# Weights of the later layers prepared within tiles 0 to 5, and rows of x loaded for the keys from GpSimd's queue

## The reference

```python
q = (x @ w_q.T).reshape(B, S, 16, 16); k = x @ w_k.T; v = x @ w_v.T      # one key and value head
attn = softmax(einsum('bshd,btd->bhst', q, k) * softmax_scale)
x = ln(x + einsum('bhst,btd->bshd', attn, v).reshape(B, S, D) @ w_out.T)
x = ln(x + gelu(x @ ternary(W1).T + b1) @ ternary(W2).T + b2)            # F = 1024; ternary: sign beyond half of mean |w|
xn = ln(x) * norm_g + norm_b; A = sigmoid(A_log)
states = A**t * cumsum((xn @ B_w.T + B_b) / max(A**t, 1e-8)); u = states @ C_w.T + C_b
h = scan over s: cat = [u_s, h]; ff1, ff2 = tanh(..); t = sigmoid(0.1 * ta + tb); h = ff1 * (1 - t) + t * ff2
x = ln(x + (x + h @ out_w.T + out_b))
x = ln(x + fp6_blocks(x) @ fp6_blocks(ffn_w).T + ffn_bias)
```

## Time and profile before

| | |
|---|---|
| median of 3 runs | 1734.12 us (1729.36 to 1743.55) |
| profiled execution | 1731.95 us, span 1730.2 us |
| busy in the span | PE 1595.8, DVE 1314.6, ACT 1240.9, POOL 1083.1 us |
| mean granted TensorE clock | 0.961 of full |
| first exponential of tiles 0, 1, 2, 3, 4, 5 | 99.1, 126.1, 146.4, 165.9, 186.1, 206.7 us |
| tiles from 12 on | 23.6 us each |

### The profile page before, as it was taken

How to read it: one execution, slowest core, us unless ns; L and a number is a source line. 1 busy time by engine, 2 the same in 40 slices (tenths; PEclk the granted TensorE clock), 3 DMA queues, 4 the chain that set the end, 5 groups by cost and what they waited for, 6 DMA issues and landing times.

```text
span 1730.2 us, 78853 instructions
## 1 busy us (share of the span) xinstructions
PE 1595.8 (92%) x32657; PEld 1129.0 (65%) x32657; DVE 1314.6 (76%) x2549; ACT 1240.9 (72%) x2343; POOL 1083.1 (63%) x3296
## 2 busy tenths in 40 slices
PE   5869989999999999999999999999999999998665
PEld 4635656676777677777667777677777677766542
DVE  5547777788888888888888888888888888884654
ACT  3426777777788777787777787777888777877321
POOL 5001235677777777777777777777777777777532
PEclk8869999999999999999999999999999999999965
DMA  9965444344433444433344433444433344420010
GB/s 235 189 91 68 63 65 59 45 73 76 76 68 63 62 75 76 75 64 61 68 76 76 75 65 58 70 75 76 76 65 62 66 76 76 76 46 22 24 30 19
DMA packets 133676, 123.75 MB, mean 72 GB/s; under 512 B 19157, under 2 KB 130825, under 8 KB 133321
## 3 DMA queue, kind: packets, MB, share of 16 engines
q1 hardware_dynamic: 129120, 118.45, 39.7%
q10 hardware_dynamic: 4200, 0.27, 0.2%
HBM read 33.73 MB, written 17.83 MB: 30 GB/s over the span
## 4 chain that ended last, share of the span: by engine, by line
PE 58%; ACT 24%; issue 5%; DVE 4%; DMA 4%; SPq 3%; POOL 2%; ACTq 0%; DVEq 0%; POOLq 0%
PE value_bank L908 11%; PE gen_bank L726 10%; PE score_banks L886 10%; ACT probs L1265 6%; PE gen_bank L733 6%; PE gate_bank L941 5%; PE max_banks L716 5%; ACT hT L1248 5%; ACT L1265 4%; ACT L1248 4%; PE gen_bank L724 3%; ACT hhi L1253 2%; ACT x L1198 2%; PE gen_bank L960 2%; PE gen_bank L950 1%
## 5 line engine op out<-in xcount | busy, mean ns | idle before, releaser
L1317 DVE TENSOR_REDUCE nmax<-max_banks 128x2 f32<-128x1024 f32 x512 | 620.7, 1212 | 77.7 <-PE max_banks L718 76.0
L1265 ACT ACTIVATE probs<-score_banks 128x1024 f32<-128x1024 f32 x512 | 522.7, 1021 | 135.1 <-PE score_banks L888 112.1
L908 PE MATMUL value_bank<-probs,vaug 128*32 128x128 f32 x8192 | 327.0, 278 | 1.6 <-ACT probs L1265 1.1
L908 PEld LDWEIGHTS value_bank<-probs,vaug 128*32 128x32 f32 x8192 | 212.6, 110 | 96.6 <-issue 74.1
L886 PE MATMUL score_banks<-qaug,kaug 64*128 64x512 f32 x512 | 249.5, 487 | 24.1 <-ACT probs L1265 17.9
L888 PE MATMUL score_banks<-qaug,kaug 64*128 64x512 f32 x512 | 249.5, 487 | 0.0
L716 PE MATMUL max_banks<-kaug,qaug 62*128 62x512 f32 x512 | 227.3, 444 | 18.6 <-DVE nmax L1317 6.6
L718 PE MATMUL max_banks<-kaug,qaug 62*128 62x512 f32 x512 | 227.4, 444 | 2.7 <-issue 2.7
L1836 POOL TENSOR_TENSOR diff<-gates 128x16 f32<-128x16 f32 x448 | 100.1, 224 | 199.3 <-ACT gates L1271 198.8
L941 PEld LDWEIGHTS gate_bank<-hseq,ghT 128*32 128x32 f32 x10944 | 141.1, 112 | 63.3 <-POOL hseq L1841 35.6
L941 PE MATMUL gate_bank<-hseq,ghT 128*32 128x16 f32 x10944 | 171.2, 185 | 3.8 <-DVE hseq L1452 1.8
(11 more groups left out here) (228 smaller groups left out, 3591.7 us busy)
## 6 DMA issues: line engine op xcount, KB each, us to landing
qstage<-qhalf SPq DMA_DIRECT2D x384, 128.0 KB
qstage<-qhalf SPq DMA_DIRECT2D x128, 112.0 KB
xt<-in_L_attn_x SPq DMA_DIRECT2D x64, 128.0 KB
xk<-in_L_attn_x SPq DMA_DIRECT2D x16, 512.0 KB, 8.2
residual<-x2s SPq DMA_DIRECT2D x64, 128.0 KB
x2f<-residual SPq DMA_DIRECT2D x64, 128.0 KB
out<-x SPq DMA_DIRECT2D x64, 128.0 KB
qaug<-nmT SPq DMA_DIRECT2D x256, 8.0 KB, 1.9
```

The source lines that it names most:

```text
L908: last = pe.matmul(value_bank[32 * g:32 * g + 32, :].rearrange("p (k t) -> p k t", k=HG)[:, :, u * BLOCK_POS:(u + 1) * BLOCK_POS], vaug[:, ...
L1265: act.activation(probs[:, beat % 2, :, :], score_banks[:, :, :], ACT.Exp).then_inc(exp_done, 1)
L1317: dve.tensor_reduce(nmax[:, m % 2, at:at + 9:8], max_banks[:, :, :], AX_X, ALU.max, negate=True).then_inc(max_taken, 1)
```

## The change

What the attention doesn't need is taken out of the setup's loop: its loads, its turns and copies, its DVE work. It is put into the engines' streams of times 0 to 5 by a new table, EARLY_AT, as (time, slot) pairs; its turned blocks go through gate_bank, which the recurrence does not use before time 8. The groups G4 to G7 (W1) are now 4 turns and one copy of 512 columns each, as are TURN0 to 3 / KEEP0 to 3 (W2). G8 to G12, SUMS, C and ROWS are the other weights, the bias sums, the product with C_w and the bias rows.

The rows of x for the keys are issued by GpSimd, between its memsets; behind the last of them GpSimd issues W1 (after xk_turned = 16), W2 (after the first maxima are placed), B_w, out_w, the gate weights, ffn_w and C_w. raw_2 takes the place of xTk in SBUF; khalf gets two buffers. The first tile's pairs stand in b = 9 to 16 and its maxima are turned, split and placed at the end of the setup. place_keys(2) and (3) move into times 0 and 1. TensorE's waits for bias_rows_made and gate_made move to the first gate input (time 7).

```diff
+EARLY_AT = dict(
+    PE=dict(MEAN1=(0, 95), G4=(1, 56), G5=(1, 78), G6=(1, 105), G7=(1, 122), MEAN2=(1, 159), TURN0=(2, 75), TURN1=(2, 126), TURN2=(2, 158), TURN3=(2, 189),
+            G8=(3, 29), G9=(3, 96), G10=(3, 143), SUMS=(4, 14), G11=(4, 68), G12=(4, 130), C=(4, 178), ROWS=(5, 25)),
+    ACT=dict(G4=(1, 61), G5=(1, 78), G6=(1, 96), G7=(1, 122), KEEP0=(2, 14), KEEP1=(2, 80), KEEP2=(2, 99), KEEP3=(2, 112),
+             G8=(3, 28), G9=(3, 53), G10=(3, 97), G11=(4, 45), G12=(4, 89), C=(4, 135), ROWS=(5, 30)),
+    DVE=dict(DECAY=(0, 40), SUM1=(0, 100), BOUNDS1=(0, 177), LESS0=(0, 184), MORE0=(0, 211), LESS1=(0, 247), MORE1=(1, 37), SUM2=(1, 99), BOUNDS2=(1, 170), LESS2=(1, 184), MORE2=(1, 232),
+             LESS3=(2, 2), MORE3=(2, 14), GATES=(2, 164), F0=(3, 70), F1=(3, 122), SUMS=(4, 50)),
+    POOL=dict(SPLIT=(4, 75)),
+    SP=dict(PLACE2=(0, 244), PLACE3=(1, 203)),
+)
...
-        group_sizes = (4, 4) + (1, 0, 0, 4, 4, 0, 4, 4, 4, 4, 4, 4, 4, 1, 4, 4, 4, 4, 0)
+        group_sizes = (4, 4, 1, 4, 4, 4, 4, 4, 4, 4, 4, 4, 1)
+        in_setup = {0: 2, 3: 3}
-        FIRST_MAX = 8
+        FIRST_MAX = 9
...
             load_x(0)
+            load_x(1)
             move_queries(0)
+            load_x(2)
+            load_x(3)
             store_keys(0)
             place_keys(0)
             store_keys(1)
+            move_queries(1)
             place_keys(1)
             store_keys(2)
             store_keys(3)
+            place_maxima(0)
             (the three bias rows)
...
+                    for name in early("SP", n, at):
+                        place_keys(int(name[5:]))
                     m = mine("NMPLACE", "MAX")
-                        if m == 0:
-                            place_keys(3)
...
@@ gpsimd, behind ident @@
+            def load_keys_x(b):
+                wait(pool, xk_turned, b - XK + 1)
+                pool.dma_start(xk[:, b % XK, :, :], x[b].rearrange("(t p) e -> p t e", p=P)).then_inc(xk_loaded[b % XK], 16)
+            for b in range(XK):
+                load_keys_x(b)
             (2 memsets of qstage)
+            (memset of vaug)
+            set_ones(0)
+            load_keys_x(4)
+            load_keys_x(5)
+            set_ones(1)
+            load_keys_x(6)
+            load_keys_x(7)
+            set_ones(2)
+            load_keys_x(8)
+            load_keys_x(9)
+            set_ones(3)
+            for b in range(10, B):
+                load_keys_x(b)
             (gate_ones, the gates' bias)
+            pool.wait_ge(xk_turned, B)
+            pool.dma_start(raw_1[:, :, :], W1.rearrange("(f p) e -> p f e", p=P)).then_inc(loaded["w1"], 16)
+            pool.wait_ge(nm_placed, 64)
+            pool.dma_start(raw_2[:, :, :], W2.rearrange("(m p) f -> p m f", p=P)).then_inc(loaded["w2"], 16)
+            (raw_b, raw_ow, raw_g, raw_f, raw_c likewise)
...
@@ tensor @@
+            turn_maxima(0)
+            pe.wait_ge(v_kept, R)
...
-            pe.wait_ge(bias_rows_made, 1)
-            pe.wait_ge(gate_made, 5)
```

More of the change, by code:

```diff
@@ L207, in tile_at, with early @@
         return m if at == place(engine, name, n) and live(m) and (kind not in ("X", "Q", "LOAD") or n - late >= 0) else None
+    def early(engine, n, at):
+        return [name for name, place in EARLY_AT[engine].items() if place == (n, at)]
     def beat_at(name, n, at):
@@ L496, in block_net @@
                 turns += [(raw_o[:, m, ks], P, P, woT[:, k, m * P:(m + 1) * P], one, ("o", 0))]
+        for f in range(FT):
+            for k in range(KT):
+                turns += [(raw_1[:, f, k * P:(k + 1) * P], P, P, w1T[:, k, f * P:(f + 1) * P], one, ("w1", 3))]
         for k in range(KT):
@@ L500, in block_net @@
             turns += [(raw_ow[:, k, :], P, P, owT[:, ks], 0.5, ("ow", 0))]
-        for f in range(FT):
-            for k in range(KT):
-                turns += [(raw_1[:, f, k * P:(k + 1) * P], P, P, w1T[:, k, f * P:(f + 1) * P], one, ("w1", 3))]
         for k in range(KT):
@@ L634, in _ @@
-            store_keys(3)
             def tile_time(c, r, n):
@@ L816, in _ @@
                     turn_values(b // GROUP - 1)
-                for i in range(2):
-                    if b == 4 + 6 * i:
-                        pe.wait_ge(setup_dve, (0, F_QUANTISED)[i] + 1)
-                        pe.matmul(gate_bank[:, 8 + i:9 + i], ones[:, :], small[:, 1 + i:2 + i], start=True, stop=True).then_inc(scale_sum, 1)
-                turn_group(2 + b)
+                if b in in_setup:
+                    turn_group(in_setup[b])
                 if b in range(SECOND, SECOND + 3):
@@ L1272, in tile_time @@
                     work(at)
+                    for name in early("ACT", n, at):
+                        prepare(name)
             run_times(act, tile_time)
@@ L1423, in _ @@
                     order_queries((b - 7) // 8)
-            for pair in range(B + MORE - FIRST_MAX, BEATS):
-                take_maxima(0, pair)
+            hold_maxima(0)
             dve.wait_ge(decay_step, DECAY_STEPS + 1)
@@ L1601, in tile_time @@
                     work(at)
+                    for name in early("DVE", n, at):
+                        prepare(name)
             run_times(dve, tile_time)
```

342 lines of the change are left out of this document (194 added, 148 removed).

## The result

| | before | after |
|---|---|---|
| median | 1731.74 us (4 runs) | 1759.51 us (4 runs, 1757.46 to 1761.48) |
| span of the profiled execution | 1730.2 us | 1755.7 us |
| mean granted clock | 0.961 | 0.959 |

A forecast was written before the change was run, and what follows sets the result against it. The setup was taken to hang on transfers and SP's one queue, later tiles on TensorE. Gain 23 (setup) - 4.4 (tile 0) - 5 (tile 1) - 7 (tiles 2 to 5) = 7 us, so 1732 - 7 = 1725 us, range 1711 to 1752.

The forecast's parts named there:

- The setup: Before the first exponential: weights and one placement leave, first exponential at 76 us instead of 99.1, a gain of 23 us.
- GpSimd's issue: Setup, loads of x on GpSimd: 1.5 us each, bounded by 0.7 and 3.0; last load issued at about 46 us.
- rival (b): Setup: GpSimd's queue becomes the pace; breaks even at 3.0 us a load, 1757 us at 4.5; chance 0.17.
- to 12.3 us nothing changes: Start of the setup: same loads and same first queries, so no change up to 12.3 us.
- the second queue: Tile 0: GpSimd's queue brings W2 and small weights beside the queries, about 9 us, of which 3 charged.
- the first keys: Setup: split at 31 us, stored at once, landed at 36, placed by 47 us where it was 56.3.
- Tile 0: Third placement lands behind tile 2's queries; tile 1 starts at about 107.5, gaining 18.6 us, so 4.4 us given back.
- Tile 1: Fourth placement behind the queries' move, needed by tile 3's pair: 5 us given back, full price 6, lower bound 3.
- Tiles 2 to 5: Moved weight work on TensorE, DVE and ACT, less TensorE's idle time: 7 us given back, bounds 3 and 15.
- (c): Setup: DVE's scalings and casts hold GpSimd's loads up, 3 to 5 us later, 1729 us in all; chance 0.08.
- (d): Bytes only displaced: third placement lands at 111, tile 1 starts 7 us earlier, 12 given back; 1736 to 1738 us; chance 0.12.

The follow-up runs named there:

- x_on_sp: Changed kernel with the 16 loads of x back on SP's queue, in the order of before; ratio 1.0094 to the kernel before, setup 82.4 us.
- before_fourth_placement_later: Kernel before with the fourth placement of keys issued behind the move of tile 2's queries, not ahead of it; 1726.18 us, ratio 0.9953.
- placements_sooner: Changed kernel with x loads on SP, third placement of keys back in the setup and fourth in tile 0; ratio 1.0089 to the kernel before.
- light_and_sooner: Changed kernel without W1's and W2's turns and copies, VectorE's weight passes on 8 columns, third placement in setup, fourth in tile 0; ratio 0.9984 to before.
- all_removed: Changed kernel: x on SP, placements sooner, W1/W2 turns and copies out, VectorE passes cut, gate-bias split, C_w product, bias rows later; ratio 0.9987 to before.
- split_and_product_later: Changed kernel with GpSimd's gate-bias split at time 6, C_w product at 5, bias rows at 7; ratio 1.0128 to before, tile 4 24.2 us.
- no_turns: Changed kernel without the 32 turns of W1 and W2 and their 8 copies, transposed buffers zero; ratio 1.0057 to the kernel before.

## Why the prediction was wrong

**The setup, 23 us forecast, 5.1 measured: the step that failed most.** It weighed GpSimd's issue with care (1.5 us a load, 0.75 measured, so rival (b) by its issue cost is refuted) and took for given "to 12.3 us nothing changes (same loads, same first queries)". The loads were the same but no longer in one queue: the first x tile landed at 13.4 us and not at 8.0. I had counted bytes that leave, and charged the second queue only 3 us, in tile 0. x_on_sp puts the price of the second queue at 11.6 us of setup: TensorE's first pair of maxima, forecast for 47 us, starts at 60.3 with x on GpSimd and at 53.2 with x on SP, and the rest of the 11.6 comes behind it, where rows of x land late (the chain has 12.70 us of one load from 59.03 on). The other 6 of the missing 18 lie ahead of that first pair. With x on SP it starts 6.2 us late and the setup ends 6.4 late; between the two lie 29.2 us, where the forecast had 29. The late part is the first keys: the forecast let their store land in 5 us and their placement in 11, where x_on_sp took 8.8 and 13.0 (first issue to last landing), and the kernel before had already taken 8.9 and 11.7.

**Tile 0, 4.4 forecast, 3.9 measured.** The size is right by luck, the split of it is not: the wait for the placement beyond the ordered queries was 1.65 us and not 6, and the landing of the queries grew by 5.2 us, with W2 and the small weights on GpSimd's queue beside it (154 GB/s in tile 0, 76 before). That these loads are what holds the queries up is likely and not shown: no run takes them alone out of tile 0. For it speaks before_fourth_placement_later, with the same order of queries and placement and no weights beside: its queries land 6.6 us after their last issue ends, the changed kernel's 13.8.

**Tile 1, 5 forecast, 5.9 measured.** The mechanism is right, and the size within what the tile varies by: placement (6.41 us when it stands alone, 6 forecast) with W1's work in its shadow, of which the forecast said that it would cost up to 6 us without that cover. placements_sooner against light_and_sooner and all_removed showed just that (28.9 and 20.9 us).

**Tiles 2 to 5, 7 forecast, 17.7 measured, outside its bounds of 3 and 15: the second step that failed.** The forecast subtracted TensorE's idle time from the added TensorE time. Idle time doesn't absorb work that stands in a chain: four turns, a copy out of the only bank, four turns; in tile 1's chain each such round is 0.9 us until ACT's copy begins, 0.60 of copy and 0.66 of turns, 2.2 us for what I had priced at 0.43 us of TensorE and a copy of 0.6 us beside it. VectorE's passes of 0.6 to 1.3 us stand between a pair's scores and its maximum, and add up to one for one (tile 3: 1.6 to 2.9 us, where 3.3 us of passes were moved in). And 3.1 of tile 4's 6.7 us came from six tiny GpSimd steps (1.5 us) and the product with C_w (1.35 us) on the one path through layer norm, store and the placing of maxima; the forecast had GpSimd's split nowhere. The other 3.6 us are TensorE's own time: 23.11 us busy where it was 19.49. Part of it is the clock, which was 1.00 in tile 4 before and 0.93 in split_and_product_later; at 0.93 some 3.4 of 24.2 us run at the lower level, which by my estimate costs 1.7 us.

**The rivals.** None gives 1759. (c), VectorE holding GpSimd up, is not seen: 15 of the 16 loads take 0.75 us, also between 20 and 40 us where VectorE works 9.67 us. By the Trainium skill's page "SBUF - State Buffer", section "Who interferes with whom", a VectorE copy, cast or tensor_scalar in a two-port mode would block GpSimd for as long as it runs; no row here shows it. The test is thin: after the first four, only three issues (at 29.39, 32.04 and 36.77 us) ran beside VectorE's work at all. (d), bytes only displaced, comes nearest: its third placement lands at 111 us, measured 116.2; tile 1 starts 1.2 us earlier where it said 7, and 23.6 us are given back in tiles 1 to 5 where it said 12.

## What to carry to other kernels

A single DMA queue is also a priority order: before moving bulk loads to a second queue, list what small transfer the start of the chain waits for, and expect it to take longer (here 1.6 to 2.2 times as long: the x tile, w_out, the queries). Don't set moved work against an engine's idle time: ask for each piece which chain it enters, through how many buffers it goes, and what is queued behind it; six tiny steps inside a layer norm and one product cost 3.1 us here, 17 matrix turns beside it at most 2.0. When two causes may cover each other, take both away in one run before crediting either; and look at the order in a queue first: swapping two entries of SP's queue in the kernel before gained more here (0.5%) than moving 3.5 MB.

## What the hardware showed that was not expected

Four loads of 128 rows of 1 KB from GpSimd went out in the same 4 KB packets as one load of 512 rows, at 0.54 us of issue each instead of 0.75. w_out's 64 byte pieces, on a third queue, ended a wait of 18.6 us beside two busy queues and 8.6 us beside one.

With zeros in weights the same instructions took less time in a later tile. Tile 9 takes 27.0 to 28.6 us in all twelve kernels with full weights, and 23.7 to 24.6 in the five with zeros, whether the zeros stand in the feed-forward weights or only in the small ones. Tile 9 of the changed kernel and of no_turns:

```profile
318.20:345.60 27.40, 24.39 (x506) 17.65 (x504) 18.85 (x33) 18.69 (x35) 15.50 (x52) 0.94 0.41 63
```

```profile
312.30:336.00 23.70, 22.95 (x506) 16.62 (x505) 18.75 (x33) 18.57 (x35) 16.60 (x52) 1.00 0.45 69
```

Both have 506 products; the one stays at the upper level of the clock, the other has a stretch at the lower. The clock is only part of it. In all twelve kernels with full weights TensorE stands idle once in this tile for 1.6 to 2.3 us, with nothing in the profile that it waits for; in the changed kernel:

```profile
329.22 0.39 PE L905 MATMUL score_banks<-qaug,kaug 64*128 64x512 f32 x1 [2.14 <-issue]
```

The lower level follows that idle time (0.59 in the stretch 330 to 334 us). None of the kernels with zeros has such a gap. Why the values of the weights should bring it about stays open. Either way, a run that leaves work out by zeros gains time in places that it doesn't mean to test.
